# Neighbourhood attention: half of the units weigh values with split 16-bit operands, the other half in 32 bit

## The reference, cut to what matters

```python
q, k, v = (qkv[0] * scale, qkv[1], qkv[2])
...
        l = jnp.einsum('bhijd,bhijd->bhij', q, kac) + bias_i[:, :, bj][None]
        logits.append(l)
attn = jax.nn.softmax(logits, axis=-1)
...
        out = out + attn[..., t, None] * vac
```

## Time and profile before

| What | Time |
|---|---|
| median of three runs | 3058.23 us |
| the profiled execution, own time | 3044.93 us |
| its span | 3043.1 us |
| mean granted clock of TensorE | 0.944 of full |

### The profile page before, as it was taken

How to read it: one execution, slowest core, us unless ns; L and a number is a source line. 1 busy time by engine, 2 the same in 40 slices (tenths; PEclk the granted TensorE clock), 3 DMA queues, 4 the chain that set the end, 5 groups by cost and what they waited for, 6 DMA issues and landing times. The chain is left out here.

```text
span 3043.1 us, 112867 instructions
## 1 busy us (share of the span) xinstructions
PE 2705.5 (89%) x31450; PEld 2390.9 (79%) x31451; DVE 2277.6 (75%) x12559; ACT 2115.7 (70%) x5724; POOL 1586.8 (52%) x2024
## 2 busy tenths in 40 slices
PE   4799999999999999999999999999909999999733
PEld 2799998899989998999899989999806766667522
DVE  2688887788878887788778878878837878877655
ACT  1588787787878787887788868888727777777400
POOL 2145555455545554555455545555635777777600
PEclk9999999999999999999999999999959999999855
DMA  2555656565556655665555555666455444444399
GB/s 50 144 119 120 127 123 125 110 125 124 124 114 124 124 125 114 122 125 123 117 122 124 123 117 123 123 122 130 102 101 97 97 95 95 96 96 94 102 323 313
DMA packets 706127, 378.50 MB, mean 124 GB/s; under 512 B 414608, under 2 KB 662064, under 8 KB 705584
## 3 DMA queue, kind: packets, MB, share of 16 engines
q1 hardware_dynamic: 652784, 235.97, 40.1%
q10 hardware_dynamic: 24192, 81.67, 9.3%
q0 software_dynamic: 28608, 54.48, 6.0%
HBM read 233.43 MB, written 98.11 MB: 109 GB/s over the span
## 5 line engine op out<-in xcount | busy, mean ns | idle before, releaser
L980 ACT ACTIVATE pr<-sc,nmx 128x100 f32<-128x100 f32 x3136 | 924.1, 369 | 61.6 <-DVE nmx L655 60.7
L890 POOL TENSOR_TENSOR oml<-om 128x256 f16<-128x256 f32 x784 | 480.4, 613 | 893.2 <-DVE om L685 877.6
L510 PE MATMUL bank<-vwin,pt 100*128 100x65 f32 x6272 | 803.8, 271 | 29.0 <-DVE om L685 28.4
L655 DVE CUSTOM_DVE_ANT_0 sc<-bank,near 128x100 f32<-128x100 f32 x3136 | 634.1, 257 | 239.0 <-PE bank L488 199.3
L510 PEld LDWEIGHTS bank<-vwin,pt 100*128 100x128 f32 x6272 | 771.0, 194 | 46.8 <-ACT pt L988 39.8
L488 PE MATMUL bank<-kimg,qexp 128*128 (+2 forms) x9408 | 627.0, 215 | 40.2 <-issue 22.2
L488 PEld LDWEIGHTS bank<-kimg,qexp 128*128 128x128 bf16 (+1 forms) x9408 | 559.9, 100 | 87.5 <-issue 55.6
L988 ACT ACTIVATE pt<-bank 100x512 f32<-100x512 f32 x784 | 461.2, 588 | 211.4 <-PE bank L497 193.5
L1347 POOL DMA_INDIRECT yrows<-ye,meta x420 | 452.9, 1078 | 173.9 <-issue 106.7
L858 POOL DMA_INDIRECT xrows<-rows,idx x448 | 425.5, 950 | 114.4 <-issue 74.3
L497 PE MATMUL bank<-cst_sb,pr 128*100 128x128 f32 x3136 | 476.1, 275 | 0.0
(11 more groups left out here) (136 smaller groups left out, 3916.6 us busy)
## 6 DMA issues: line engine op xcount, KB each, us to landing
vwin<-v_pix SPq DMA_DIRECT2D x1120, 60.5 KB
near<-bias_rows ACTq DMA_DIRECT2D x112, 600.0 KB, 4.9
y<-yrows SPq DMA_DIRECT2D x112, 224.0 KB, 4.2
qexp<-qring SPq DMA_DIRECT2D x896, 14.0 KB
v_pix<-vrow SPq DMA_DIRECT2D x56, 225.8 KB
xin<-in_x SPq DMA_DIRECT2D x56, 224.0 KB
xres<-in_x SPq DMA_DIRECT2D x112, 112.0 KB
x<-xres SPq DMA_DIRECT2D x112, 112.0 KB
```

The source lines that it names most:

```text
L510: mm = pe.matmul(ps_av[m % 2][:, 2 * t + blk, :], pt[:, m % 2, 2 * t + blk, :], vwin[:, st, 2 * u + t, 64 * blk:64 * blk + 65], start=True ...
L655: i = v.tensor_tensor_reduce(out=sc[:, ring(m, par), k, :], in0=ps_s[m % 2][:, k, :], in1=near[:, st, ct, k, :], scale=-1.0, scalar=-MASKE ...
L890: g.tensor_tensor(oml[:, st, u], om[:, st, u], om_h[:, st, u], ALU.subtract).then_inc(s["oml_done"], 1)
L980: i = a.activation(pr[:, r, k, :], sc[:, r, k, :], ACT.Exp, bias=nmx[:, r, k:k + 1], scale=-1.0)
```

## The change

Units m = 0, 3, 4, 5, 7, 10 and 12 of each pair (`SPLIT`) weigh with twelve 16-bit products in place of four fp32 ones. The upper half of each word of `pt` serves as bf16 upper part of the probability in place; GpSimd writes the remainder as fp16 into a new tile `pl`. A pixel's row of values grows from 129 to 194 words (`VP`): the 129 words as before, whose upper halves serve as bf16, and behind them 129 fp16 remainders, which VectorE writes into `vrow` (`a_v_l`, at step 12). All units' windows are loaded with 194 words. The exponentials are written over `sc`; `pr` is gone. `L_V`, `L_P`, `L_H` and `L_F` are one step more, so that the weighing comes five steps behind the scores, and the fold is in steps 0 and 7. `true_gap` moves from VectorE (step 11) to GpSimd (step 8), and GpSimd's scatters move to other steps.

```diff
-L_T, L_V, L_P, L_H, L_F = 3, 4, 5, 6, 7
+L_T, L_V, L_P, L_H, L_F = 3, 5, 6, 7, 8
+SPLIT = (0, 3, 4, 5, 7, 10, 12)
+VP = VW + VW // 2 + 1
...
-        vwin = asb("vwin", [NKEY, 2, NTILE, VW])
+        vwin = asb("vwin", [NKEY, 2, NTILE, VP])
+        vwin_h = vwin[:].bitcast(BF16)[:, :, :, 1:2 * VW:2]
+        vwin_l = vwin[:].bitcast(FP16)[:, :, :, 2 * VW:3 * VW]
...
-        pr = asb("pr", [128, RING, 4, NKEY])
...
+        pl = asb("pl", [NKEY, 2, 4, 128], FP16)
+        pt_h = pt[:].bitcast(BF16)[:, :, :, 1::2]
...
                 def weigh(J, m, par):
                     n = UPP * J + m
                     st, u = divmod(m, UNITS)
-                    pe.wait_ge(s["th_done"], n + 1)
+                    if m in SPLIT:
+                        pe.wait_ge(s["t_out"], len(SPLIT) * J + SPLIT.index(m) + 1)
+                    else:
+                        pe.wait_ge(s["th_done"], n + 1)
...
+                            if m in SPLIT:
+                                p_h, p_l = pt_h[:, m % 2, 2 * t + blk, :], pl[:, m % 2, 2 * t + blk, :]
+                                v_h, v_l = vwin_h[:, st, 2 * u + t, cols], vwin_l[:, st, 2 * u + t, cols]
+                                for k, (a_, b_) in enumerate(((p_h, v_h), (p_h, v_l), (p_l, v_h))):
+                                    mm = pe.matmul(at_, a_, b_, start=k == 0, stop=k == 2)
+                            else:
+                                mm = pe.matmul(at_, pt[:, m % 2, 2 * t + blk, :], vwin[:, st, 2 * u + t, cols], start=True, stop=True)
...
+                def a_v_l(I):
+                    v.wait_ge(s["v_h"], I + 1)
+                    for blk in range(2):
+                        cols = slice(65 * blk, 65 * blk + 64)
+                        i = v.tensor_tensor(vrow_l[:, :, cols],
+                                            ps_a[0:HALF, :].rearrange("p (n c) -> p n c", n=NROW)[:, :, 64 * blk:64 * blk + 64],
+                                            vrow_h[:, :, cols], ALU.subtract)
+                    i.then_inc(s["v_out"], 1)
...
                 def add_bias(J, m, par):
...
-                        v.wait_ge(s["exp_done"], n - RING + 1)
+                        v.wait_ge(s["t_done"], n - RING + 1)
...
-                R_STEPS = {5: (moments,), 6: (spreads, choose), 7: (rank,), 9: (pick_two,), 11: (true_gap, places), 13: (shares,)}
+                R_STEPS = {5: (moments,), 6: (spreads, choose), 7: (rank,), 9: (pick_two,), 11: (places,), 13: (shares,)}
...
-                LATE_STEPS = {9: a_q_l, 10: a_k_l}
+                LATE_STEPS = {9: a_q_l, 10: a_k_l, 12: a_v_l}
...
+                    g.wait_ge(s["r_gap"], c + 1)
+                    if not early(c, 1):
+                        g.wait_ge(s["r_eg"], 2 * c)
+                    g.tensor_tensor(gapr[:], gap[:], rs[:, par], ALU.mult).then_inc(s["r_gapr"], 1)
...
-                SCATTERS = {0: (0, 0), 2: (0, 1), 3: (0, 2), 5: (0, 3), 6: (1, 0), 9: (1, 1), 10: (1, 2), 12: (1, 3)}
+                SCATTERS = {0: (0, 0), 1: (0, 1), 2: (0, 2), 4: (0, 3), 5: (1, 0), 9: (1, 1), 11: (1, 2), 12: (1, 3)}
...
+                def split_t(J, m, par):
+                    n = UPP * J + m
+                    g.wait_ge(s["th_done"], n + 1)
+                    g.tensor_tensor(pl[:, m % 2], pt[:, m % 2], pt_h[:, m % 2], ALU.subtract).then_inc(s["t_out"], 1)
...
                             if reached(J, m, L_H):
                                 split_l(*back(J, m, par, L_H))
+                            if reached(J, m, L_T) and (m - L_T) % UPP in SPLIT:
+                                split_t(*back(J, m, par, L_T))
...
-                    i.then_inc(s["v_out"], 1)
+                    i.then_inc(s["v_h"], 1)
...
-                        i = a.activation(pr[:, r], sc[:, r], ACT.Exp)
+                        i = a.activation(sc[:, r], sc[:, r], ACT.Exp)
```

More of the change, by code:

```diff
@@ L103, in sem @@
             return ctx.enter_context(nc.semaphore(name))
-        v_pix = nc.dram_tensor("v_pix", (B * IMG, VW), FP32, kind="Internal").ap()
+        v_pix = nc.dram_tensor("v_pix", (B * IMG, VP), FP32, kind="Internal").ap()
         bias_rows = nc.dram_tensor("bias_rows", (3, 128, 3 * 4 * NKEY), FP32, kind="Internal").ap()
@@ L216, in build @@
         names = """w_in w_scaled w1_in cst_in rpb_in pad_out gath_in turned win_in bias_done zeroed pad_zero
-            x_in mean_done xc_done sq_done sub_done th_done oml_done
+            x_in mean_done xc_done sq_done v_h sub_done th_done oml_done
             var_done ve_done root_done spread_done xn_done q_done q_h q_out k_done k_h k_out v_done v_out v_store q_exp0 q_exp1
-            v_in0 v_in1 s_done max_done exp_done t_done av_done rec_done orec_done om_done
+            v_in0 v_in1 s_done max_done exp_done t_done t_out av_done rec_done orec_done om_done
             o_done o_out proj_done proj_out bias_out near_in0 near_in1 xres_in0 xres_in1 x1_store0 x1_store1
@@ L496, in transposes @@
                     for k in range(4):
-                        mm = pe.transpose(ps_t[m % 2][0:NKEY, k * 128:(k + 1) * 128], pr[:, ring(m, par), k, :], ident)
+                        mm = pe.transpose(ps_t[m % 2][0:NKEY, k * 128:(k + 1) * 128], sc[:, ring(m, par), k, :], ident)
                     mm.then_inc(s["t_done"], 1)
@@ L731, in pick_two @@
                     v.tensor_tensor(hots[:, par], hot[:, par, 0], hot[:, par, 1], ALU.add).then_inc(s["r_hots"], 1)
[L733 to L736, removed]
                 def places(c, par):
@@ L910, in _ @@
                     split_l(*back(PAIRS, m, PAIRS % 2, L_H))
+                    if m < L_T and (m - L_T) % UPP in SPLIT:
+                        split_t(*back(PAIRS, m, PAIRS % 2, L_T))
                 for Q in range(PAIRS - 3, PAIRS):
@@ L976, in exps @@
                     if subtracted(m):
-                        i = a.activation(pr[:, r], sc[:, r], ACT.Exp)
+                        i = a.activation(sc[:, r], sc[:, r], ACT.Exp)
                     else:
                         for k in range(4):
-                            i = a.activation(pr[:, r, k, :], sc[:, r, k, :], ACT.Exp, bias=nmx[:, r, k:k + 1], scale=-1.0)
+                            i = a.activation(sc[:, r, k, :], sc[:, r, k, :], ACT.Exp, bias=nmx[:, r, k:k + 1], scale=-1.0)
                     i.then_inc(s["exp_done"], 1)
```

18 lines of the change are left out of this document (11 added, 7 removed).

## The result

The changed kernel takes 3350.32 us in the median of four runs (3320.72 to 3370.90), beside 3058.53 us for the kernel before in the same series: **ratio 1.0925, 95% interval 1.0852 to 1.0999**, so slower by about 9%. The forecast was 3000 us, with a range of 2945 to 3060. The execution that left the profile is the slowest of the four, 3370.90 us with a span of 3369.1; the ratio leaves it out and compares the other three.

What follows compares the result with a forecast made beforehand. PE bounds the kernel at 37.2 us a pair; afterwards the SP loop would, at 36.1. 48 x 1.1 = 53 us, plus 10 at rounds, less small losses: net 58 off 3044.93, 2987; with 13.3 for the median, 3000 us (2945 to 3060).

Steps and rivals of the forecast that it cites:

- Wider rows: Windows' transfers with 776-byte pieces in place of 516: mostly hidden behind SP's issue, 0.4 us taken (0 to 1.2).
- The ring: Loop of scores, steps to the weighing, SP's windows, spread, next scores: becomes the bound at 36.1 us a pair; 50%.
- rival 2: Wider rows back up SP's issue and slow the loop past 37.2 us a pair: up to 38.1, 3096 us; 14%.
- its sign: In SP's queue, the spread's issue would start over 9 us after the windows.
- Rival 5: PE's clock falls after waits of about 1 us a pair: over 3100 us; 2%.
- The weighing: On PE, a split unit's twelve 16-bit products take 0.45 us in place of 0.84, saving 2.7 us a pair.
- rival 4: The weights' load shows in PE's split products: 1.2 us in place of 0.84, 3185 us; 3%.
- PE alone: PE sets the pace because the spread lands earlier than added up: 34.9 us a pair, 2953 us; 20%.
- rival 1: PE sets the pace, the spread landing earlier: 34.9 us a pair, 2953 us, or 2925 with cheaper products; 20%.
- Other engines: New work on POOL (8.3 us a pair) and DVE: 0.4 us a pair on PE's path, hidden in its spread wait.
- rival 3: DVE or POOL fall behind and delay PE: 36.6 to 37 us a pair, 3015 to 3045 us; 10%.

Runs made afterwards that it cites:

- e8: Changed kernel with ScalarE's load of the next pair's bias issued in step 10 in place of step 7; 3221.66 us, ratio 1.0537.
- e1: Changed kernel with each transfer of a strip's inner tiles taking one key column in place of one key row; 3401.27 us, ratio 1.1119.
- e3: Changed kernel with windows loading only 129 of the 194 words, the values' remainders left zero; 3030.65 us, ratio 0.9909.
- e6: Changed kernel with 14 idle fp32 products on TensorE before step 0's wait for the spread; 3364.64 us, ratio 1.1005.
- e11: Changed kernel with spread transfers between window rows, residual and token loads moved into strip 0's windows, and windows loading 129 of 194 words; 2953.82 us.
- e4: Kernel before with only the weighing and all behind it one step later, no split or wide rows; 3030.60 us, ratio 0.9903.

## Why the prediction was wrong, point by point

**The step that failed is "Wider rows".** It took 0.4 us a strip (0 to 1.2) because "issuing a strip's windows takes 7 us, longer than the transfer, so most hides". Three things in it were wrong.
- *The price of a piece.* q1's packets took 1573 - 1220 = 353 us more per engine. If all of that is the windows', 353 x 16 / (56 x 2,800) = 36 ns for 260 bytes. Counted by size in the traces, a piece took 45.8 ns before and 75.8 after, so 30 ns, where a line through two unlike queues gave 13.5. Nor do the traces show 16 engines on them: for more than half of the time that wide pieces are in flight, ten to twelve are. By 11 at a time, an estimate of 1,400 x 75.8 / 11 = 9.6 us a strip, over the 6.6 of its issue, and of 5.8 before. So 1.2 us more was no upper bound. Part of the price is company: with the bias moved away (e8) a piece takes 68.6 ns. In e1 it takes 49.4, for a reason that stays open. The Trainium skill ("Advanced Engine Details and Errata", DMA Bandwidth Details) says that SBUF is reached by 16 ports of 27.2 GB/s, each tied to eight partitions; ten partitions then lie on two of them at least, an estimate of 54 GB/s at the least. e1 agrees in direction; no run here isolates a port.
- *The cover.* The transfer was set against its own issue alone, and no row showed that "issue is longer than transfer". The engines were already 0.78 to 0.84 busy while the narrow windows landed, and half as many bytes again, with the bias now earlier in their tail, did not fit. The 0.62 of the earlier trace rows is the mean of a pair. e8 shows what the sharing cost.
- *Who pays.* The windows' own issue did stay at 6.6 us, as predicted (that it goes with the pieces alone does not hold: e1 has the same pieces). The overhang fell on the spread behind: 19.3 - 14.5 = 4.8 us of issue, and landing took 1041.22 - 1038.45 = 2.8 where 2.0 was added.

**The ring** was the right mechanism. From the weighing's end (the start of the product behind it) to the scores it took 1041.22 - 1011.64 = 29.6 us, against 24.2 predicted and 25.3 as the point where rival 2 decides. Rival 2 is what happened, but its largest case was 26.2, and its sign did not show: the spread's issue starts 1019.15 - 1012.28 = 6.9 us after the windows, not over 9, since the back-up stands in the spread's own issue. e3 has the forecast's wait of about 1.5 us in 28 pairs, once the width is gone; that its 3030.65 us lie in the range is in part luck, since the shift, which the sum did not have, gives as much alone.

**Rival 5** was set apart with 2%, yet it hangs on rival 2. A wait of 6.28 us lowers the clock, so steps 0 to 4 take 1056.28 - 1041.22 = 15.1 us where 11.9 was predicted. 29.6 + 15.1 = 44.7, the pair of the timeline (1085.90 - 1041.22). Of the 8.6 us over the forecast 5.4 are the transfer's and 3.2 the clock's, as this pair adds up; over its run e6 did not get the 3.2 back. The prediction had no case in which one rival sets off the other. Over the attention the split should have saved 7 x (0.84 - 0.38) x 48 = 155 us of PE's time, and PE was busy 31 us more: an estimate of some 186 us of work drawn out by the clock, beside 322 - 64 = 258 us of more idle time.

**The weighing** was right, a little dear: 0.38 us a unit against 0.45, 32 ns a product, at the lower end of 25 to 52. The 81 ns that the Trainium skill gives for 128 columns ("TensorE: Matmul & The Clock Gate", Back-to-back issue gap) do not show in this stream of 65; rival 4 is out.

**PE alone** at 34.9 us a pair (rival 1) is near what e11 shows, 35.0, but e11 needs another order of SP's queue besides narrow rows.

**Other engines.** The groups by line and shape, 300 to 2300 us:

```profile
L917 POOL TENSOR_TENSOR pl<-pt 100x512 f16<-100x512 f32 x320 | 332.8, 1040 | 490.9 <-ACT pt L1025 490.6
...
L665 DVE TENSOR_TENSOR vrow<-bank,vrow 112x256 f16<-112x256 f32 x90 | 34.0, 420 | 3.0 <-ACT vrow L989 1.0
```

1.04 us for `split_t` against 1.16 and 0.42 for the subtraction against 0.43; POOL's 27.0 us a pair against 28.2. Right in size, and off the path in the kernel after. Where the path is freed (e11), short waits for VectorE take back part of the gain, which is rival 3 in small.

**The shift** was costed only in the ring. Alone it gained 0.97% (e4), and the prediction had no term for it.

**Sums.** Two times of the rivals do not follow from their own terms, and nothing hangs on them: with 0.30 us a weighing rival 1 comes to 2953 - 7 x 0.15 x 48 = 2903, not 2925, and rival 3 at 36.6 us a pair to 3000 + 0.5 x 48 = 3024, not 3015.

## What to carry to other kernels

A transfer hides behind its own issue only if the DMA engines have room in those very microseconds: read their share in stretches of a few microseconds, and count everything in flight there, not the mean of a period. Price a longer piece from pieces of the same transfers, by the number of engines that these keep busy, and look at who is next in the queue, because the overhang is paid there. When a rival ends in a long wait of TensorE, add what its clock then costs, and give the pair of them a chance of their own.

## What the runs showed of the hardware that was not expected

- Pieces of 776 bytes took 75.8 ns each where those of 516 took 45.8; with the bias load moved away 68.6 (e8), and with partitions ten apart, read from ten image rows and issued half as fast, 49.4 (e1).
- The same transfers in the form of e1 took twice as long to issue, 9.68 us for ten in place of 4.59.
- After waits of 6.2 to 6.3 us TensorE ran near the lower clock level for about 9 us (scores 1.23 us in place of 0.8), with 0.55 of full granted; with products in that gap the scores behind it took 0.91 and then 0.79 us (e6).
